# Batch 3's token sums by full-precision products, and batches 2 and 3 finished inside the first pair

## The chip, the cores and the metric

The kernel runs on one core of one Trainium2 chip. The metric is the device time of one execution in microseconds, median over runs. A core has five engines with a queue each: TensorE (PE in the rows, its weight loads PEld), VectorE (DVE), ScalarE (ACT), GpSimd (POOL), and SyncE (SP), which here issues the transfers. Each engine runs its own instructions strictly in program order and waits on semaphores.

## What is computed

An attention-like stage made of two int8-style quantised products adds to the residual `x`; then comes a mixture of experts in which the whole launch picks two of eight experts:

```python
x = x + xattn(layernorm(x), fside, ctx)      # x: 4 batches x 512 tokens x 512
n = layernorm(x).reshape(-1, 512)            # 2048 tokens
router_logits = n @ gate_w.T                 # 8 experts
_, sel = top_k(router_logits.sum(axis=0), 2) # ONE choice for all tokens
rw = softmax(router_logits[:, sel], axis=1)
h = gelu(einsum('nd,kdf->knf', n, w1[sel]) + b1[sel])
y = einsum('knf,kfd->knd', h, w2[sel]) + b2[sel]
x = x + einsum('nk,knd->nd', rw, y)
```

The choice needs the sum of all 2048 normalised tokens, and no expert weight can be fetched before it.

## The kernel before

Everything is written out by hand: for each engine a list of calls in the order in which its queue holds them. There is no scheduler.

**First stage** (to about 130 us): the quantised products of the four batches, b = 0 to 3. Then, per batch, second-layernorm moments (`moments(b, 2)`), the inverse root and minus mean times root on GpSimd (`inv_std`, L337), and four normalised tiles of 128 tokens: batch 2's by GpSimd (`normalise(2)`, L393), of batch 3 two by ScalarE and two by VectorE (`normalise_last`). TensorE transposes them (`normed2(b, h)`, 8 transposes of 128x128 each, L656) into PSUM slots `y.b.h`. Draining a slot also yields that batch's token sums, by an accumulating copy on ScalarE (`keep_full`) or by a reduction on VectorE (`token_sums`, L1334). `keep_hi` and `keep_lo` (L973, L1291) split the transposed batch into two rounded parts, whose sum is exact enough for three-product matmuls.

**Choice**: `token_total` (L1342) adds the sums of all batches; `expert_sums` (L677, 4 full-precision products with a right side of 8 columns) and `choose_experts` (L1346 to L1349) give `top_i`. SyncE reads it and issues the load of the first weights (L285, L289). ScalarE and VectorE split them (`first_weights`: a_hi L985, a_lo L1381), `pick_experts` and `pick_bias` (L1353 to L1375) select bias columns. `router(b)` (L667, 8 products of 512 columns) gives batch b's logits.

**Pairs**: an expert's hidden layer is cut into 8 parts; 16 pairs (expert, part) follow. Each handles the tokens in two halves, tp = 0 (batches 0, 1) and tp = 1 (batches 2, 3). In the first pair each half has four tiles `plain(tp, n)` (12 products each, L850), gelu on ScalarE, its low part on GpSimd (L476), and four `down` groups (12 products each, L805), drained by VectorE with the routing weights `rw` (L1541). In half 0 the logits of all batches are turned (`logit_columns`, L685) between tile 1 and tile 2; from them VectorE and GpSimd make `rw` (`pick_logits`, the power at L523, `token_weights`). Later pairs use a seven-product scheme (L792); they are not touched.

PSUM slots are handed on by a written table, `SLOT_USES`: a use may be filled when the use before it in its row is drained.

Of the kernel before, what the change touches and what calls it, by code (L numbers as in the profile page):

```python
# [14 lines left out]
P = 128  # L15
# [8 lines left out]
def xattn_ffn(  # L24
# [37 lines left out]
    with ExitStack() as ctx:  # L62
# [6 lines left out]
        def each(name):  # L69
# [43 lines left out]
        tok_sum = sb("tok_sum", [P, KD, B])  # L113
# [114 lines left out]
        part_ready, tok_ready, t4_sum = each("part_ready"), sem("tok_ready"), sem("t4_sum")  # L228
# [89 lines left out]
        def _(pool):  # L318
# [24 lines left out]

            def emptied(use):
                i, n = place(use)
                pool.wait_ge(drained[i], n + 1)
# [46 lines left out]
            def normalise(b):  # L393
                pool.wait_ge(nmr_ready[b], 2)
                for j in range(TT):
# [73 lines left out]
            normalise(2)  # L469
            inv_std(3, 2)  # L470
# [70 lines left out]
        def _(pe):  # L541
# [105 lines left out]
            def normed2(b, h):  # L647
                ps, full = fill(f"y.{b}.{h}")
                for j in range(TT):
                    if b == B - 1 and j >= H:  # L650
                        pe.wait_ge(xn_last, j - H + 1)
                    else:
                        pe.wait_ge(xn2_ready[b], j + 1)
# [18 lines left out]

            def expert_sums():
                pe.wait_ge(tok_ready, 1)
# [100 lines left out]
            normed2(3, 0)  # L775
            normed2(3, 1)
            router(1)
            expert_sums()
            router(0)
            router(2)  # L780
            router(3)
# [73 lines left out]
            def first_pair():  # L855
                for tp in range(2):
# [3 lines left out]
                    plain(tp, 0)  # L860
                    plain(tp, 1)
                    if tp == 0:
                        pe.wait_ge(drained[1], ALL_DRAINED[1])
                        for b in range(B):
                            logit_columns(b)
                    plain(tp, 2)
# [22 lines left out]
        def _(act):  # L889
            s = nc.scalar  # L890

            def normalise(b, c):
                act.wait_ge(nmr_ready[b], c)
                for j in range(H if c == 2 and b == B - 1 else TT):
                    s.activation(xv[b][:, j, :], res[:, b * TT + j, :], ACT.Identity, bias=nmr[c - 1][b][:, j:j + 1],
                                 scale=rstd[c - 1][b][:, j:j + 1]).then_inc(xn_ready[b] if c == 1 else xn2_ready[b], 1)

# [67 lines left out]
            def keep_summed(b, h):  # L965
                ps, empty = drain(f"y.{b}.{h}")
                act.wait_ge(part_ready[b], 1)
# [110 lines left out]
            keep_full(1, 1)  # L1078
            keep_hi(1, 0)
            keep_hi(1, 1)  # L1080
            keep_hi(0, 0)
            keep_hi(0, 1)
            normalise(3, 2)
            keep_full(2, 0)
            keep_full(3, 0)
            keep_summed(2, 1)
            keep_hi(2, 0)
            keep_hi(2, 1)
            keep_summed(3, 1)
            keep_hi(3, 0)  # L1090
            keep_hi(3, 1)
# [5 lines left out]
            keep_logits(2)  # L1097
            keep_logits(3)
# [527 lines left out]
```

## Time and profile before

| | us |
|---|---|
| median of 3 runs | 820.6 (820.12, 820.6, 821.82) |
| span of the profiled execution | 818.7 |
| TensorE busy in it | 771.5 (94%) |
| VectorE, GpSimd, ScalarE busy | 477.7, 449.7, 354.6 |
| mean granted TensorE clock | 0.979 |

The profiled execution's own device time is not listed apart from the three runs; its span, from first to last instruction, is 1.9 us under their median. Busy shares are means over stages with different limits: TensorE is 94% busy over the whole, but in the last 10 us before the choice of experts it is not. The change touches only the stretch from about 128 to 177 us.

### The profile page before, as it was taken

The page shows a single profiled execution, that of the slowest core. Times are in us where ns is not written, and L with a number is a line of the kernel's source. Part 1 is how long each engine was busy: PE and PEld are TensorE (multiplying, and loading weights), DVE is VectorE, ACT ScalarE, POOL GpSimd, SP SyncE. Part 2 cuts the span into 40 slices and gives each one's busy share as a digit, 9 for nine tenths or more (in the row PEclk, how much of TensorE's full clock was granted, in tenths as well). Part 3 has the DMA queues.
Part 4 walks back from the last instruction along what each step waited for, and adds up shares of the span by engine and source line. Part 5 has one row for each costly group of instructions (what it writes and reads, how often), then busy time and mean ns, then how long its engine had stood idle before and what let it go on. Part 6 is the DMA issues. An engine that isn't in the chain of part 4 may idle for free.

```text
span 818.7 us, 11342 instructions
## 1 busy us (share of the span) xinstructions
PE 771.5 (94%) x3570; PEld 624.1 (76%) x3577; DVE 477.7 (58%) x669; ACT 354.6 (43%) x660; POOL 449.7 (55%) x497
## 2 busy tenths in 40 slices
PE   5688666999999999999999999999999999999998
PEld 4666455688788888888888888888888888888886
DVE  5999759797754545454545454545454545454545
ACT  3967588743442434343424343434343434242422
POOL 1789997157564646464646464646464646464622
PEclk9899968999999999999999999999999999999999
DMA  9400000301010101010101010101010101010022
GB/s 344 173 2 1 1 0 2 129 1 51 1 52 1 51 0 49 3 50 2 48 4 51 1 45 6 42 9 44 7 41 11 36 15 36 15 32 19 0 103 104
DMA packets 19077, 32.34 MB, mean 39 GB/s; under 512 B 872, under 2 KB 11240, under 8 KB 18160
## 3 DMA queue, kind: packets, MB, share of 16 engines
q1 hardware_dynamic: 18896, 31.98, 11.1%
q8 instruction: 12, 0.20, 0.1%
q10 hardware_dynamic: 160, 0.08, 0.0%
q14 instruction: 9, 0.07, 0.0%
HBM read 27.87 MB, written 4.19 MB: 39 GB/s over the span
## 4 chain that ended last, share of the span: by engine, by line
PE 83%; POOL 8%; DVE 3%; issue 2%; ACT 2%; DMA 1%; ACTq 0%; POOLq 0%; DVEq 0%
PE slot L805 42%; PE slot L792 34%; PE slot L850 3%; POOL wv L366 2%; POOL xf L383 1%; PE slot L667 1%; POOL wv L372 1%; POOL cv L366 1%; PE slot L585 1%; DVE rmax L1226 1%; DMA b_rows<-in_L_ffn_b 1%; POOL rstd L340 1%; POOL h_lo L476 1%; DVE stats L1217 1%; DVE peak_x L1226 1%
## 5 line engine op out<-in xcount | busy, mean ns | idle before, releaser
L792 PE MATMUL slot<-xo,a_hi 128*128 128x512 f32 x840 | 259.1, 390 | 0.0
L1541 DVE SCALAR_TENSOR_TENSOR res<-slot,rw,res 128x512 f32<-128x512 f32 x256 | 178.5, 750 | 130.3 <-PE slot L805 130.2
L1570 DVE TENSOR_TENSOR e<-slot,e 128x512 f32<-128x512 f32 x150 | 103.8, 692 | 173.4 <-PE slot L792 173.3
L805 PE MATMUL slot<-w_hi,h_hi 128*128 128x512 f32 x512 | 201.3, 393 | 0.4 <-POOL h_lo L476 0.4
L805 PE MATMUL slot<-w_lo,h_hi 128*128 128x512 f32 x512 | 199.6, 390 | 0.0
L805 PE MATMUL slot<-w_hi,h_lo 128*128 128x512 f32 x512 | 199.4, 390 | 0.0
L792 PEld LDWEIGHTS slot<-xo,a_hi 128*128 128x128 f32 x840 | 157.4, 188 | 33.3 <-DVE e L1570 0.2
L476 POOL TENSOR_TENSOR h_lo<-e,h_hi 128x512 fp32r<-128x512 f32 x96 | 138.1, 1451 | 55.0 <-ACT e L1104 54.0
L792 PE MATMUL slot<-xo,a_lo 128*128 128x512 f32 x420 | 163.7, 390 | 0.0
L805 PEld LDWEIGHTS slot<-w_hi,h_hi 128*128 128x128 f32 x512 | 96.1, 188 | 25.1 <-POOL h_lo L476 5.6
L476 POOL TENSOR_TENSOR h_lo<-hid,h_hi 128x512 fp32r<-128x512 f32 x32 | 44.1, 1378 | 124.7 <-ACT hid L1104 124.7
L805 PEld LDWEIGHTS slot<-w_hi,h_lo 128*128 128x128 f32 x512 | 96.2, 188 | 20.1
L805 PEld LDWEIGHTS slot<-w_lo,h_hi 128*128 128x128 f32 x512 | 96.2, 188 | 19.3
L792 PEld LDWEIGHTS slot<-xo,a_lo 128*128 128x128 f32 x420 | 78.9, 188 | 16.5
L1103 ACT ACTIVATE h_hi<-e,b_now 128x512 fp32r<-128x512 f32 x90 | 64.9, 721 | 58.0 <-DVE e L1570 57.6
L1142 ACT COPY e<-slot 128x512 f32<-128x512 f32 x30 | 17.6, 587 | 164.5 <-PE slot L792 164.5
L490 POOL TENSOR_TENSOR a_lo<-raw,a_hi 128x256 fp32r<-128x256 f32 x45 | 34.3, 761 | 95.9 <-ACT a_hi L988 95.9
L991 ACT CAST w_hi<-raw 128x512 fp32r<-128x512 f32 x32 | 19.8, 622 | 109.8 <-PE slot L805 109.8
L495 POOL TENSOR_TENSOR w_lo<-raw,w_hi 128x512 fp32r<-128x512 f32 x30 | 38.7, 1289 | 50.4 <-ACT w_hi L991 50.4
L1104 ACT ACTIVATE e<-e,b_now 128x512 f32<-128x512 f32 x90 | 63.8, 709 | 0.0
L1103 ACT ACTIVATE h_hi<-slot,b_now 128x512 fp32r<-128x512 f32 x38 | 26.2, 689 | 66.5 <-PE slot L792 56.6
L490 POOL TENSOR_TENSOR a_lo<-ssum,a_hi 128x256 fp32r<-128x256 f32 x60 | 43.7, 739 | 0.0
(145 smaller groups left out, 814.5 us busy)
## 6 DMA issues: line engine op xcount, KB each, us to landing
raw<-in_L_ffn_w SPq DMA_DIRECT2D x32, 512.0 KB, 3.4
res<-in_x SPq DMA_DIRECT2D x4, 1024.0 KB, 11.9
wv<-in_fside_BxS2xS SPq DMA_DIRECT2D x4, 1024.0 KB, 12.8
out_x<-res SPq DMA_DIRECT2D x3, 1024.0 KB, 3.9
cv<-in_ctx SPq DMA_DIRECT2D x4, 512.0 KB, 13.1
out_x<-res SPq DMA_DIRECT2D x4, 256.0 KB, 2.7
b_row<-in_L_ffn_b SPq DMA_DIRECT2D x2, 256.0 KB, 4.6
b_rows<-in_L_ffn_b ACTq DMA_DIRECT2D x1, 64.0 KB, 6.0
```

What stands on the lines that cost most here:

```text
L366: g.tensor_tensor(w[:, j, :], w[:, j, :], rows[b][:, 0:n], ALU.mult).then_inc(wmul_ready[b], 1)
L476: g.tensor_tensor(h_lo[:, i, :], hid[i][:, :], h_hi[:, i, :].bitcast(F32), ALU.subtract).then_inc(h_ready, 1)
L490: g.tensor_tensor(a_lo[:, i, :, :], A_OF[i], a_hi[:, i, :, :].bitcast(F32), ALU.subtract).then_inc(a_ops_ready, 1)
L495: g.tensor_tensor(w2_lo[:, f, :], raw2[:, f, :], w2_hi[:, f, :].bitcast(F32), ALU.subtract).then_inc(w2_ready, 1)
L792: last = t.matmul(dst, a[:, i, k, :], xo[tp][:, v, k, :], start=(start and n == 0), stop=(n == 3 * H - 1), skip_group_check=True)
L805: last = t.matmul(y_bank[j][:, :], a[:, i, j * P:(j + 1) * P], v[:, f, :], start=(start and n == 0), stop=(not start and n == 2), skip_gro ...
L850: last = t.matmul(TILE_BANK[n], a[:, 2 * f + h, k, :], xo[q][:, v, k, :], start=(m == 0), stop=(m == 3 * KD - 1))
L991: s.copy(w2_hi[:, f, :], raw2[:, f, :]).then_inc(w2_hi_ready, 1)
L1103: s.activation(h_hi[:, i, :], src, ACT.Gelu_apprx_tanh, bias=bias).then_inc(hid_ready, 1)
L1104: s.activation(hid[i][:, :], src, ACT.Gelu_apprx_tanh, bias=bias).then_inc(hid_ready, 1)
L1541: v.scalar_tensor_tensor(out=r, in0=y_bank[j][:, :], scalar=rw[:, ds(p, 1), n:n + 1].rearrange("p a b -> p (a b)"), in1=r, op0=ALU.mult, o ...
L1570: v.tensor_tensor(dst[:, :], src, other[:, :], ALU.add).then_inc(comb_ready, 1)
```

## The change

1. Batch 3's token sums no longer wait for its transposes. The sum over tokens of (residual x root − mean x root) is formed by `last_sums`: for each of 4 token tiles and 4 feature blocks one full-precision product with the residual block as the stationary side and the column of roots as the moving side (16 products of 1 column, L697 in the new file), and one product of ones with the shifts (L694).
2. Batch 3's moments and roots come in two halves (`moments_last`, `inv_std_last`). Of batch 2's normalised tiles GpSimd makes two, ScalarE the other two (`normalise_half`).
3. `normed2(3, *)`, `router(2)` and `router(3)` move from before the choice into half 0 of the first pair; `logit_columns` moves behind `router(3)`, one tile later. The drains, splits and copies that belong to them move too on ScalarE and VectorE.
4. VectorE picks experts and bias, and normalises its two tiles of batch 3, before the first weights' low parts instead of after them.

```diff
- "a.2 s2.0 p2.0.1 y.3.1 r.3 "),
+ "a.2 s2.0 p2.0.1 t e r.1 "),
...
+def inv_std_last(h):
+    b, at = B - 1, slice(H * h, H * h + H)
+    pool.wait_ge(var_ready[b], 2 + h)
+    g.tensor_tensor(rstd[1][b][:, at], var_e[1][b][:, at], neg_half[:, at], ALU.pow).then_inc(rstd_last, 1)
+    pool.wait_ge(rstd_last, h + 1)
+    g.tensor_tensor(nmr[1][b][:, at], nmean[1][b][:, at], rstd[1][b][:, at], ALU.mult
+                    ).then_inc(nmr_ready[b], 1)
...
-def normalise(b):
+def normalise(b, h):
     pool.wait_ge(nmr_ready[b], 2)
-    for j in range(TT):
+    for j in range(H * h, H * h + H):
...
 inv_std(2, 2)
-normalise(2)
-inv_std(3, 2)
+normalise(2, 0)
+inv_std_last(0)
+inv_std_last(1)
...
+        elif b == B - 2 and j >= H:
+            pe.wait_ge(xn_acts, j - H + 1)
...
+def last_sums(h):
+    b = B - 1
+    ps, full = fill("t") if h == 0 else (slot[place("t")[0]], filled[place("t")[0]])
+    pe.wait_ge(rstd_last, h + 1)
+    for j in range(H * h, H * h + H):
+        if h == 1 and j == TT - 1:
+            pe.wait_ge(nmr_ready[b], 3)
+            t.matmul(ps[:, 0, KD:2 * KD], ones[:, :], nmr[1][b][:, :], start=True, stop=True,
+                     skip_group_check=True)
+        for k in range(KD):
+            last = t.matmul(ps[:, 0, k:k + 1], res[:, b * TT + j, k * P:(k + 1) * P],
+                            rstd[1][b][:, j:j + 1], start=(j == 0), stop=(j == TT - 1),
+                            skip_group_check=True)
+    if h == 1:
+        last.then_inc(full, 1)
 def expert_sums():
-    pe.wait_ge(tok_ready, 1)
     ps, full = fill("e")
     for k in range(KD):
...
-normed2(3, 0)
-normed2(3, 1)
-router(1)
+last_sums(0)
+last_sums(1)
 expert_sums()
 router(0)
-router(2)
-router(3)
+router(1)
...
         plain(tp, 0)
+        if tp == 0:
+            normed2(3, 0)
+            normed2(3, 1)
         plain(tp, 1)
         if tp == 0:
             pe.wait_ge(drained[1], ALL_DRAINED[1])
+            router(2)
+        plain(tp, 2)
+        if tp == 0:
+            router(3)
             for b in range(B):
                 logit_columns(b)
-        plain(tp, 2)
         pe.wait_ge(hid_ready, 8 + 8 * tp + 2)
         plain(tp, 3)
...
+def normalise_half(b):
+    act.wait_ge(nmr_ready[b], 2)
+    for j in range(H, TT):
+        s.activation(xv[b][:, j, :], res[:, b * TT + j, :], ACT.Identity, bias=nmr[1][b][:, j:j + 1],
+                     scale=rstd[1][b][:, j:j + 1]).then_inc(xn_acts, 1)
...
-    act.wait_ge(part_ready[b], 1)
+    if b == 2:
+        act.wait_ge(part_ready, 1)
...
+keep_hi(0, 0)
+normalise_half(2)
+keep_hi(0, 1)
+keep_full(2, 0)
 keep_hi(1, 0)
 keep_hi(1, 1)
-keep_hi(0, 0)
-keep_hi(0, 1)
 normalise(3, 2)
-keep_full(2, 0)
-keep_full(3, 0)
 keep_summed(2, 1)
-keep_hi(2, 0)
-keep_hi(2, 1)
-keep_summed(3, 1)
-keep_hi(3, 0)
-keep_hi(3, 1)
 keep_logits(0)
 keep_logits(1)
 first_weights(0, 2)
 first_weights(2, 4)
 s.activation(gelu_warm[:, :], half[:, 0:1], ACT.Gelu_apprx_tanh)
-keep_logits(2)
-keep_logits(3)
-first_down_weights()
+keep_hi(2, 0)
+keep_hi(2, 1)
...
             gelu(0, n, TILES[n][0], TILE_BANK[n])
+            if tp == 0 and n == 0:
+                keep_summed(3, 0)
+                keep_summed(3, 1)
+            if tp == 0 and n == 1:
+                keep_hi(3, 0)
+                keep_hi(3, 1)
+                first_down_weights()
+                keep_logits(2)
+            if tp == 0 and n == 2:
+                keep_logits(3)
...
+def moments_last(h):
+    b, at = B - 1, slice(H * h, H * h + H)
+    for j in range(H * h, H * h + H):
+        if h == 0:
+            dve.wait_ge(res_added[b], j + 1)
+        else:
+            dve.wait_ge(res_last, j - H + 1)
+        ins = v.bn_stats(stats[b][:, j, :], res[:, b * TT + j, :])
+    link(ins)
+    for j in range(H * h, H * h + H):
+        ins = v.bn_aggr(mv[b][:, j, :], stats[b][:, j, :])
+    link(ins)
+    v.tensor_scalar(nmean[1][b][:, at], mv[b][:, at, 0], -1.0, None, ALU.mult)
+    v.tensor_scalar(var_e[1][b][:, at], mv[b][:, at, 1], LN_EPS, None, ALU.add).then_inc(var_ready[b], 1)
...
+def early_total():
+    for b in range(B - 1):
         emptied(f"y.{b}.0")
     for b in range(2):
         emptied(f"y.{b}.1")
-        dve.wait_ge(part_ready[2 + b], 1)
-    v.tensor_reduce(tok_total[:, :], tok_sum[:, :, :], AX.X, ALU.add).then_inc(tok_ready, 1)
+    dve.wait_ge(part_ready, 1)
+    link(v.tensor_reduce(tok_early[:, :], tok_sum[:, :, :], AX.X, ALU.add))
+def token_total():
+    ps, empty = drain("t")
+    link(v.tensor_reduce(tok_shift[:, :], ps[:, 0, KD:2 * KD], AX.X, ALU.add))
+    v.scalar_tensor_tensor(out=tok_total[:, :], in0=ps[:, 0, 0:KD], scalar=tok_shift[:, 0:1],
+                           in1=tok_early[:, :], op0=ALU.add, op1=ALU.add).then_inc(empty, 1)
...
 moments(2, 2)
+moments_last(0)
 add_last_residual()
-moments(3, 2)
+moments_last(1)
+token_sums(2)
+early_total()
 keep_lo(0, 0)
-keep_lo(1, 0)
-normalise_last()
-token_sums(2)
-keep_lo(1, 1)
-token_sums(3)
 token_total()
 keep_lo(0, 1)
 choose_experts()
+normalise_last()
+keep_lo(1, 0)
+keep_lo(1, 1)
+pick_experts()
+pick_bias()
+first_weights(0, 2)
+first_weights(2, 4)
 keep_lo(2, 0)
 keep_lo(2, 1)
-keep_lo(3, 0)
-keep_lo(3, 1)
-first_weights(0, 2)
-first_weights(2, 4)
-pick_experts()
-pick_bias()
-first_down_weights()
-pick_logits()
...
     last_operands(0)
+    keep_lo(3, 0)
+    keep_lo(3, 1)
+    first_down_weights()
     fourth_operand(0)
+    pick_logits()
     token_weights()
```

Three places of the written order follow. First TensorE, from the end of batch 2's transposes to the choice: before, in this piece, batch 3's last transposes (slot1), `router(1)` and the expert product.

```order
L656 MATMUL slot1<-ident,xf1 128x128 [waits xn_last]
L656 MATMUL slot1<-ident,xf1 128x128
L667 MATMUL slot2<-xo0,gwt 16x512 [waits lo_ready1,drained2]
L667 MATMUL slot2<-xo0,gwt 8x512
...
L677 MATMUL slot3<-gwt_full,tok_total 128x8 [waits drained3,tok_ready]
L677 MATMUL slot3<-gwt_full,tok_total 128x8 x3
```

And now, at the same place (L697 and L694 are `last_sums`, L706 the expert product, L681 `router(0)`):

```order
L697 MATMUL slot1<-rstd2_3,res 128x1 [waits rstd_last,drained1]
L697 MATMUL slot1<-rstd2_3,res 128x1 x7
L697 MATMUL slot1<-rstd2_3,res 128x1 [waits rstd_last]
L697 MATMUL slot1<-rstd2_3,res 128x1 x3
L694 MATMUL slot1<-nmr2_3,ones 128x4 [waits nmr_ready3]
L697 MATMUL slot1<-rstd2_3,res 128x1 x4
L706 MATMUL slot1<-gwt_full,tok_total 128x8 [waits drained1]
L706 MATMUL slot1<-gwt_full,tok_total 128x8 x3
L681 MATMUL slot0<-xo0,gwt 16x512 [waits lo_ready0,drained0]
```

The transposes of batch 3 and one router are gone from ahead of the expert product, and 17 products stand there.

Second, VectorE between the choice (MAX_INDEX writes `top_i`) and the first weights' low parts (`a_lo`), before:

```order
L1349 MAX_INDEX top_i<-top_v,sum_row 128x8 [waits dve_link]
L1291 TENSOR_TENSOR xo1<-xf1,xo1 128x1024 [waits hi_ready2] x2
L1291 TENSOR_TENSOR xo1<-xf1,xo1 128x1024 [waits hi_ready3] x2
L1381 TENSOR_TENSOR a_lo<-raw1,a_hi 128x256 [waits a_hi_ready] x4
L1353 CAST top_f<-top_i 128x8 [waits top_ready]
```

and now:

```order
L1414 MAX_INDEX top_i<-top_v,sum_row 128x8 [waits dve_link]
L1382 TENSOR_SCALAR xf1<-res,rstd2_3,nmr2_3 128x512 [waits nmr_ready3]
L1382 TENSOR_SCALAR xf1<-res,rstd2_3,nmr2_3 128x512
L1350 TENSOR_TENSOR xo0<-xf0,xo0 128x1024 [waits hi_ready1] x2
L1418 CAST top_f<-top_i 128x8 [waits top_ready]
L1420 TENSOR_SCALAR onehot<-iota,top_f 128x16 [waits dve_link] x2
L1438 TENSOR_TENSOR picked<-b1_all,onehot 128x16x8 [waits dve_link]
L1440 TENSOR_REDUCE b1_col<-picked 128x16 [waits dve_link]
L1438 TENSOR_TENSOR picked<-b1_all,onehot 128x16x8 [waits dve_link]
L1440 TENSOR_REDUCE b1_col<-picked 128x16 [waits dve_link]
L1446 TENSOR_TENSOR a_lo<-raw1,a_hi 128x256 [waits dve_link,a_hi_ready]
```

Four splits stood there; now two normalised tiles, two splits (`keep_lo(1, *)`, which `router(1)` needs) and seven small instructions stand there.

Third, TensorE in half 0 of the first pair, behind its first tile (L877 is `plain`, L670 `normed2(3, *)`, L681 `router(2)`, L714 `logit_columns`), now:

```order
L877 MATMUL slot0<-xo0,a_lo 128x512
L670 MATMUL slot2<-ident,xf1 128x128 [waits xn2_ready3,drained2]
...
L877 MATMUL slot0<-xo0,a_hi 128x512 [waits lo_ready0,a_ops_ready]
...
L681 MATMUL slot2<-xo1,gwt 16x512 [waits lo_ready2,drained2,drained1]
...
L877 MATMUL slot1<-xo0,a_hi 128x512 [waits lo_ready1,a_ops_ready]
...
L681 MATMUL slot3<-xo1,gwt 16x512 [waits lo_ready3,drained3]
...
L714 MATMUL slot1<-ident,logits 128x16 [waits drained3]
```

Before, only the logit columns stood between the tiles of this half.

## Rows read from the trace of the kernel before

**Rows 1.** The page: shares of the chain that ended last, by engine.

```profile
PE 83%; POOL 8%; DVE 3%; issue 2%; ACT 2%; DMA 1%; ACTq 0%; POOLq 0%; DVEq 0%
```

**Rows 2.** Chain of waits, 136 to 177 us: start us, us, what.

```profile
136.63 1.94 POOL rstd L340
...
139.89 3.87 PE slot L656 x16
143.75 2.79 PE slot L667 x8
...
147.34 1.87 PE slot L667 x8
...
149.29 2.14 PE slot L667 x8
...
153.71 5.47 PE slot L850 x24
...
160.28 5.69 PE slot L850 x24
165.97 10.88 PE slot L805 x48
```

**Rows 3.** Windows, TensorE alone: stretch, length, busy, granted clock.

```profile
132.00:135.40 3.40, 0.66 (x4) 1.00 0.00 0
135.40:138.80 3.40, 3.00 (x14) 0.51 0.00 0
138.80:142.20 3.40, 2.59 (x12) 0.50 0.01 2
142.20:145.60 3.40, 3.40 (x13) 0.50 0.00 0
```

**Rows 4.** The same view of an earlier stretch.

```profile
16.00:19.40 3.40, 3.31 (x16) 0.50 0.99 387
```

**Rows 5.** Timeline of TensorE: start us, us, engine line op out<-in xcount.

```profile
123.27 1.09 PE L656 MATMUL slot<-ident,xf 128*128 128x128 f32 x8
...
135.90 3.18 PE L656 MATMUL slot<-ident,xf 128*128 128x128 f32 x12 [0.30 <-POOL xf L396]
...
139.89 3.87 PE L656 MATMUL slot<-ident,xf 128*128 128x128 f32 x16 [0.81 <-ACT xf L895]
...
146.38 0.95 PE L677 MATMUL slot<-gwt_full,tok_total 128*128 128x8 f32 x8
```

**Rows 6.** Timeline of VectorE, 138 to 157 us.

```profile
138.93 1.00 DVE L1323 TENSOR_SCALAR xf<-res,rstd,nmr 128x512 f32<-128x512 f32 x2
...
145.24 1.22 DVE L1291 TENSOR_TENSOR xo<-xf,xo 128x1024 fp32r<-128x1024 f32 x1
...
147.86 0.16 DVE L1349 FIND_INDEX8 top_i<-top_v,sum_row 128x8 uint32<-128x8 f32 x1
...
152.60 1.43 DVE L1381 TENSOR_TENSOR a_lo<-raw,a_hi 128x256 fp32r<-128x256 f32 x4
153.95 0.17 DVE L1353 CAST top_f<-top_i 128x8 f32<-128x8 uint32 x1
...
155.84 0.29 DVE L1375 TENSOR_REDUCE b_col<-picked 128x16 f32<-128x128 f32 x1
```

**Rows 7.** Timeline of ScalarE, 133 to 155 us.

```profile
133.00 3.89 ACT L973 CAST xo<-xf 128x1024 fp32r<-128x1024 f32 x4
138.93 1.52 ACT L895 ACTIVATE xf<-res,nmr,rstd 128x512 f32<-128x512 f32 x2 [2.04 <-POOL nmr L341]
...
149.24 1.05 ACT L982 COPY logits<-slot 16x512 f32<-16x512 f32 x2 [0.30 <-PE slot L667]
152.16 1.33 ACT L985 CAST a_hi<-raw 128x256 fp32r<-128x256 f32 x4 [1.87 <-DMA raw<-in_L_ffn_w]
```

**Rows 8.** Timeline of GpSimd: the power for the routing weights.

```profile
162.69 2.90 POOL L523 TENSOR_TENSOR lpow<-euler,lsub 128x16 f32<-128x16 f32 x1 [0.84 <-DVE lsub L1366]
```

**Rows 9.** Timeline of VectorE: the first outputs with routing weights.

```profile
170.07 2.73 DVE L1541 SCALAR_TENSOR_TENSOR res<-slot,rw,res 128x512 f32<-128x512 f32 x4
```

More of the change, by code:

```diff
@@ L112, in xattn_ffn @@
         logits = sb("logits", [2 * E, B, T])
-        tok_sum = sb("tok_sum", [P, KD, B])
+        tok_sum = sb("tok_sum", [P, KD, B - 1])
+        tok_early = sb("tok_early", [P, KD])
+        tok_shift = sb("tok_shift", [P, 1])
         tok_total = sb("tok_total", [P, KD])
@@ L227, in xattn_ffn @@
         res_last, xn_last = sem("res_last"), sem("xn_last")
-        part_ready, tok_ready, t4_sum = each("part_ready"), sem("tok_ready"), sem("t4_sum")
+        part_ready, t4_sum = sem("part_ready"), sem("t4_sum")
+        rstd_last, xn_acts = sem("rstd_last"), sem("xn_acts")
         tsum_ready = [sem(f"tsum_ready{tp}") for tp in range(2)]
@@ L1320, in normalise_last @@
                 b = B - 1
-                dve.wait_ge(nmr_ready[b], 2)
+                dve.wait_ge(nmr_ready[b], 3)
                 for j in range(H, TT):
@@ L1333, in token_sums @@
                 ps, _ = drain(f"y.{b}.1")
-                v.tensor_reduce(tok_sum[:, H:2 * H, b], ps[:, :, :], AX.X, ALU.add).then_inc(part_ready[b], 1)
-            def token_total():
-                for b in range(B):
+                v.tensor_reduce(tok_sum[:, H:2 * H, b], ps[:, :, :], AX.X, ALU.add).then_inc(part_ready, 1)
+            def early_total():
+                for b in range(B - 1):
                     emptied(f"y.{b}.0")
```

6 rows, old and new, of the table SLOT_USES are left out of this document.

## The prediction, on record before the result

> **What bounds the kernel now.** I read the page first: the chain that ended last lies on TensorE for 83% of the span [rows 1]. So work on TensorE counts wherever it does not fall into a gap. The chain in order of time comes next [rows 2]. The reader is to see three pieces. Until 139.89 us the chain is on GpSimd: batch 3's inverse root, 136.63 to 138.57, and then the normalised tiles that wait for it. From 139.89 to 153.71 it is all TensorE: 16 transposes of batch 3, router(1), the expert product, the other three routers. From 153.71 to 176.85 it is TensorE again: the four tiles of the first pair's half 0 and its four down groups. In this last piece nothing else shows, so what is moved into it lengthens it by its full duration.
>
> Third, the clock [rows 3]. TensorE was granted its full 2.4 GHz until 135.4, fell to 1.2 GHz after a stretch in which it worked 0.66 of 3.40 us, and stayed there to 145.6, although it was busy for 3.00, 2.59 and 3.40 us of the three stretches that follow. Batch 3's transposes therefore cost 3.87/16 = 0.242 us each [rows 5], against 1.09/8 = 0.136 at full clock.
>
> Fourth, how the first weights arrive. The choice is known at 147.86 + 0.16 = 148.02 [rows 6], the weights are there and ScalarE starts on them at 152.16 [rows 7], 4.14 us later, and the low parts start at 152.60. A first tile could start at about 153.3; router(3) ends at 153.71. So weights and TensorE are late together, by 0.4 us, and to gain anything both must come earlier.
>
> **The change, step by step.** I follow the path to the first tile (call its start W), then what is put behind it.
>
> *Batch 2's transposes.* Now GpSimd makes four tiles and the last transposes run to 135.90 + 3.18 = 139.08 [rows 5]. ScalarE takes two of them behind one split of 3.89/4 = 0.97 us from 133.00, at 1.52/2 = 0.76 each: ready at 135.5 instead of 136.6 [rows 7]. Twelve transposes at 0.242 from about 135.4 end at 138.3. Gain 0.8 us.
>
> *Batch 3's roots.* VectorE makes the second half's moments about 1 us later than now, GpSimd has two tiles fewer ahead; the power took 1.94 us for four columns [rows 2] and cannot take longer for two, so the roots are there by 138.9. TensorE is in the first half of the sums until later than that. No wait.
>
> *The token sums.* 16 + 1 full-precision products. The expert product shows the kind: 4 products are 8 records and 0.95 us, 0.119 us a pass at full clock [rows 5]; at half clock I take the 0.242 of a transpose, which also loads 128 columns. 34 passes are 4.0 us at full clock and 8.2 at half. This is the disputed price. At full clock from the start the sums end at 142.4, at half to the end at 146.5. Which clock? The rows speak both ways: in an earlier stretch TensorE did nothing but transposes for 3.3 of 3.4 us at half clock [rows 4] and was at full clock right after it; from 135.4 to 143.7 it did transposes nearly without a pause and was not [rows 3]. No row shows a stream of 1-column products. I take the middle, a clock that comes back halfway: 6.1 us, end at 144.4.
>
> The Trainium skill (TensorE: Matmul & The Clock Gate, Why this matters for your kernels) says that keeping TensorE continuously busy is what brings the full clock. By that rule the sums, which are dense, run at full clock nearly from their start, the first of the rivals below; rows 4 agree with it, the stretch 138.8 to 143.7 in rows 3 does so poorly. The same page (LDWEIGHTS) lets a weight load cost its columns, whatever the product behind it is: 128 columns give 107 ns, so that 34 loads would be an estimated 3.6 us for products of a single column. The 0.119 us a pass beside an 8-column product agrees. It speaks against this form of the sum: with the residual as the stationary side the cost is all loading.
>
> *From the sums to the choice.* Two small VectorE instructions with their gaps, 0.45: 144.9. Expert product 0.95: 145.8. From there to the index the row of before needs 148.02 − 147.33 = 0.7 [rows 5, 6]: 146.5. Against 148.02 that is 1.5 us earlier. The weights land 4.14 later, at 150.7.
>
> *From the choice to the first tile.* The weights are not what comes last now. VectorE's queue holds ahead of the first low part: batch 3's two tiles 1.00, two splits of 1.22, and the picks, 153.95 to 156.13 or 2.2 us [rows 6]; together 5.6 us, to 152.1. Behind them two low parts at 1.43/4 = 0.36, and a semaphore: W = 153.0. On ScalarE the high parts wait behind the logits of router(1), whose operands VectorE has ready at 150.0; router 2.14 us at most [rows 2], copy 0.5, high part 0.33 [rows 7]: also 152 to 153. So W comes 0.7 us earlier than 153.71, and 5.6 us of VectorE's list eat the earlier choice.
>
> *What is moved behind W.* 16 transposes at 0.136: 2.2 us, if the clock is full there. Two routers at 2.14 [rows 2]: 4.3 us. Logit columns wait for the copy of the last logits, 1.05/2 = 0.52 [rows 7] and two hand-overs, while before they had been drained: 0.6. Sum 7.1 us. Cover: none, the chain there is TensorE without a break.
> The batch 3 drains, splits and copies now in ScalarE's and VectorE's lists run beside tiles 1 and 2 and the routers (2 x 2.14 + 2 x 2.73 us); their sum on ScalarE is about 6 us with a gelu of 1.3 between. Cost nothing, 0.5 at most if router(3) waits for its low part. GpSimd's low parts of the hidden tiles stand ahead of later down groups and have time.
>
> *Routing weights.* Logit columns stand one tile later. From the end of the columns at 160.28 to the first output at 170.07 it took 9.8 us [rows 2, 9], of which the power is 2.90 [rows 8]. TensorE needs the first drained bank after a tile and two down groups, 5.69/2 + 10.88/2 = 8.3 us, less now than before (11.1). VectorE has no operand sums left between pick and weights, which cost over 3 us there; I take 7.9 to 9.4 and a stall of 0.2 (0 to 1.1).
>
> **Sum.** Start of down: 153.0 + (165.97 − 153.71 = 12.26) + 7.1 = 172.4, against 165.97: +6.4. With the stall +6.6. SyncE's queue has the same entries. Nothing later is touched: the chain goes on with 10.88 us of down groups and follows TensorE. Span 818.7 + 6.6 = 825.3; the median stands 1.9 above the span, so 820.6 + 6.6 = 827.2; I say 827.0.
>
> **Rivals.**
> *R1, full clock through the sums.* They end at 142.5 to 142.8, W at 151.3, the rest as above: +4.7, 825.3. For it: rows 4, and less waiting ahead of batch 2's last transposes. Against it: three stretches of rows 3.
> *R2, half clock until the routers.* Sums 8.2 us, expert product 1.9: the choice at 149.6, later than before, so the change doesn't do what it says; W = 156.1, and the first tile may still run slowly. +9.7, 830.3. For it: in rows 3 the clock came back only once routers had run for over 2 us (from 143.7), and now nothing wide runs between 138.3 and the choice. Against it: rows 4.
> *R3, not slower.* Mechanism: the early choice pays in full. Choice at 142.1 with the clock never lost, the landing 4.14 later rather than VectorE's list setting W, and low parts at once: W = 147.0, +0.4 net of the 7.1: 821.0 or, with no wait for logits, 820.4. It decides from W below 153.71 − 7.1 = 146.6. VectorE's 5.6 us of list speak against it, and they are in the written order.
> *R4, another wait,* such as router(3) behind its split or the third down group behind the weights by more than 1 us: +1 to +2 on any of these.
>
> **How the numbers follow.** About 0.2% (1.6 us) is what a measurement here tells from no change. Forecast (clock back within the sums) 0.42; R1 0.22; R2 0.26; R3 0.08, half of it below −1.6 us or so through something not seen; R4 alone 0.02. The forecast's own range is 825.3 to 829. The whole range must take in R1 and most of R2: 823.5 to 831. Slower 0.92, same 0.04, faster 0.04.
>
> **What would show it.** The granted clock from 138 to 146, and the length of the block of 1-column products: 4.0, 6.1 or 8.2 us. The index at 146.5, the first a_lo at about 152.2 with its wait on VectorE's own queue and not on the transfer. W near 153. Then in half 0 transposes of 2.2 us and two routers of 2.1 us on the chain, between the tiles, and the down groups from 172.4. Wrong would be: a chain that leaves TensorE in half 0, sums under 4 us, or W below 150.

## The result, and the profile after

| | before | after |
|---|---|---|
| median of 4 runs each, us | 821.21 (820.12 to 821.84) | 827.39 (826.95 to 829.17) |
| span of the profiled execution, us | 818.7 | 825.4 |
| TensorE busy in it, us | 771.5 | 776.5 |
| mean granted TensorE clock | 0.979 | 0.977 |

The change is slower: ratio 1.0089, 95% interval [1.0076, 1.0103]. The medians stand 6.2 us apart, which alone would be 1.0075, at the lower end of the interval; the spans of the two profiled executions stand 6.7 apart. In a second set of runs the ratio was 1.0105 [1.0083, 1.0126].

The shares of the chain are nearly those of [rows 1]; VectorE has gained a point, and we will see where:

```profile
PE 82%; POOL 8%; DVE 4%; issue 3%; ACT 2%; DMA 1%; ACTq 0%; POOLq 0%; DVEq 0%
```

The chain of waits of the changed kernel over the stretch of [rows 2] (start us, us, what):

```profile
135.98 3.16 PE slot L670 x14
139.14 2.82 PE slot L697 x24
...
143.59 1.88 PE slot L706 x8
145.47 5.75 PE slot L681 x16
...
152.87 2.99 PE slot L877 x12
155.86 1.75 PE slot L670 x16
...
160.35 1.85 PE slot L681 x8
...
164.94 1.85 PE slot L681 x8
166.78 1.11 PE slot L714 x16
...
170.36 2.91 POOL lpow L535
...
176.86 0.76 DVE res L1603
177.76 5.70 PE slot L832 x24
```

Read it against [rows 2] at two places. The first tile of the pair starts at 152.87 instead of 153.71: that is the whole yield of the early choice, 0.84 us. Its half 0 now holds 1.75 us of transposes and 1.85 + 1.85 us of routers. The down groups start at 170.7 instead of 165.97. And the chain leaves TensorE behind the logit columns (L714): it reaches the third down group over GpSimd's power and VectorE's small steps to `res`. Before, it did not.

Windows of TensorE in the changed kernel (stretch, length, busy and count, granted clock), to stand beside [rows 3]:

```profile
135.40:138.80 3.40, 2.82 (x14) 0.61 0.03 5
138.80:142.20 3.40, 3.40 (x30) 0.89 0.01 2
142.20:145.60 3.40, 2.89 (x17) 0.61 0.00 0
145.60:149.00 3.40, 3.40 (x9) 0.50 0.23 60
```

The full clock came back at about 139.5, early in the block of sums, and was lost again at about 142.9, although TensorE had been busy for all of 138.8 to 142.2. So the 8 records of the expert product took 1.88 us instead of the 0.95 of [rows 5], and `router(0)` began at 1.2 GHz.

Timeline of TensorE after, the wait at the third down group (in brackets the idle time ahead and what ended it):

```profile
177.76 0.47 PE L832 MATMUL slot<-w_hi,h_hi 128*128 128x512 f32 x1 [1.45 <-DVE res L1603]
```

TensorE waits here for a bank that VectorE drains with the routing weights. The row shows 1.45 us of idle time. But the end of a product's record overlaps with the start of the next. Two down groups take 5.44 us, half of the 10.88 in [rows 2], so the third was due at 170.70 + 5.44 = 176.14 and started 1.62 us late; 1.62 is the figure used below. Timeline of VectorE after, to stand beside [rows 6, 9]:

```profile
145.99 0.16 DVE L1414 FIND_INDEX8 top_i<-top_v,sum_row 128x8 uint32<-128x8 f32 x1
...
152.16 1.43 DVE L1446 TENSOR_TENSOR a_lo<-raw,a_hi 128x256 fp32r<-128x256 f32 x4 [0.76 <-ACT a_hi L1025]
...
173.36 1.27 DVE L1581 TENSOR_TENSOR lexp<-lpow,is_top 128x16 f32<-128x16 f32 x2 [2.91 <-POOL lpow L535]
174.55 1.26 DVE L1582 TENSOR_SCALAR lden<-lpow 128x16 f32<-128x16 f32 x1
```

And of GpSimd:

```profile
173.22 2.56 POOL L488 TENSOR_TENSOR h_lo<-e,h_hi 128x512 fp32r<-128x512 f32 x2
```

`lexp` (two instructions) and `lden` work on 128x16 values. The first `lexp` took 0.16 us, the second 1.18 and `lden` 1.26. They lie exactly beside two low parts (`h_lo`) on GpSimd, subtractions with two inputs, 1.28 us each.

This hold-up is not new. The kernel before has it too, though TensorE did not wait there (timelines of VectorE and of GpSimd before; L1295 and L1310 are operand sums):

```profile
162.82 2.49 DVE L1295 TENSOR_TENSOR xf<-xf 128x1024 f32<-128x1024 f32 x2
165.34 1.23 DVE L1310 TENSOR_TENSOR xf<-xf 128x1024 f32<-128x1024 f32 x1
166.60 1.24 DVE L1519 TENSOR_TENSOR lexp<-lpow,is_top 128x16 f32<-128x16 f32 x2
167.76 1.26 DVE L1520 TENSOR_SCALAR lden<-lpow 128x16 f32<-128x16 f32 x1
```

```profile
165.56 3.43 POOL L476 TENSOR_TENSOR h_lo<-e,h_hi 128x512 fp32r<-128x512 f32 x2
```

### The profile page after: what moved, and what is told of

It reads as the page before. It is cut to its first block, busy times and chain, and to the rows that moved or that the text cites. A ratio compares the mean times of both kernels' runs of the same rounds, so it can differ in the third digit from the quotient of the medians.

```text
span 825.4 us, 11412 instructions
## 1 busy us (share of the span) xinstructions
PE 776.5 (94%) x3604; PEld 629.5 (76%) x3611; DVE 477.9 (58%) x672; ACT 355.5 (43%) x659; POOL 448.6 (54%) x497
## 4 chain that ended last, share of the span: by engine, by line
PE 82%; POOL 8%; DVE 4%; issue 3%; ACT 2%; DMA 1%; ACTq 0%; POOLq 0%; DVEq 0%
PE slot L832 41%; PE slot L819 33%; PE slot L877 2%; POOL wv L377 2%; PE slot L681 1%; POOL xf L394 1%; POOL wv L383 1%; POOL cv L377 1%; DVE rmax L1285 1%; PE slot L597 1%; DMA b_rows<-in_L_ffn_b 1%; POOL h_lo L488 1%; PE slot L670 1%; DVE stats L1261 1%; DVE peak_x L1285 1%
```

## The experiments

After the prediction's result three things were open: whether the wait for the routing weights is what the rows suggest; what decides TensorE's clock around the sums; and which part of the change costs the 6 us. Every ratio below is against the kernel before, run on the same chip in the same set. That kernel's median was 821.21, 819.47, 820.01 and 819.87 us in the four sets, so times of different sets are compared by their ratios.

### Low part ahead of the power

In `first_pair` on GpSimd:

```diff
                 hid_lo(0, 0, 1)
+                hid_lo(0, 0, 2)
                 pool.wait_ge(lsub_ready, 1)
                 g.tensor_tensor(lpow[:, :], euler[:, :], lsub[:, :], ALU.pow).then_inc(lexp_ready, 1)
-                hid_lo(0, 0, 2)
+                pool.wait_ge(y_free, TT + 1)
                 hid_lo(0, 0, 3)
```

> The changed kernel with one edit on GpSimd: the third hidden tile's low part goes ahead of the power for the routing weights, the fourth waits until the first output of the pair is drained, so that nothing of GpSimd's runs beside VectorE's small instructions that make the weights. Theory (the wait of the third down group is made by GpSimd's two subtracts running beside lexp and lden, 1.27 and 1.26 us instead of about 0.3 each): the weights are ready 1.8 us earlier, TensorE's gap before the third down group (176.1 to 177.8) closes, and the kernel gains 1.6 us: 825.8. Rival (those two instructions are slow of themselves, or the power alone is late): the gap stays, 827.4, or 1 us worse since the fourth low part now comes late.

Measured: 825.76 us, ratio 1.0073 [1.0056, 1.009], against 1.0089 and 1.0105 of the changed kernel. VectorE's timeline:

```profile
174.90 0.26 DVE L1582 TENSOR_TENSOR lexp<-lpow,is_top 128x16 f32<-128x16 f32 x2 [2.91 <-POOL lpow L536]
175.07 0.17 DVE L1583 TENSOR_SCALAR lden<-lpow 128x16 f32<-128x16 f32 x1
```

With nothing beside it on GpSimd, `lden` takes 0.17 us, not 1.26, and TensorE waits nowhere between 165 and 190. The intervals of the ratios overlap, so the times alone would not prove the gain; that the wait is gone, and why, the trace shows.

### The block of sums twice

```diff
             last_sums(0)
+            last_sums(1, False)
+            last_sums(0)
             last_sums(1)
```

The 17 added products compute the same sums once more.

> The changed kernel with batch 3's sums formed twice in a row on TensorE (17 full-precision products more, the same result). It prices the block and shows its clock. Theory A (weight loads beside 1-column products do not keep the full clock, it was lost at 142.8 after 3.4 us of them): the first block runs as before, the second wholly at half clock, 34 passes x 0.24 = 8 us, and the time rises by about 8 us, 835.5. Theory B (a busy TensorE keeps its clock): 34 x 0.12 = 4 us, 831.4, granted clock 1.0 from 139.4 on.

Measured: 835.99 us, ratio 1.0199 [1.018, 1.0218]; the span is 7.7 us longer than the changed kernel's (833.1 against 825.4), as theory A had it. Timeline and windows of TensorE:

```profile
139.47 2.98 PE L697 MATMUL slot<-rstd,res 128*128 128x1 f32 x24
142.53 6.20 PE L697 MATMUL slot<-rstd,res 128*128 128x1 f32 x32
...
149.03 1.84 PE L697 MATMUL slot<-rstd,res 128*128 128x1 f32 x8
```

```profile
142.20:145.60 3.40, 3.40 (x23) 0.67 0.00 0
145.60:149.00 3.40, 3.40 (x17) 0.50 0.00 0
149.00:152.40 3.40, 2.89 (x14) 0.50 0.00 0
```

The first 24 records cost 0.124 us each, the last 8 cost 0.230: 1.2 GHz. The clock came back at about 140.0, within the first block, and was lost at about 143.4, just before the second block began (about 143.6). TensorE was busy without a break on both sides of that moment, so a pause there is not what takes the clock away. The second block, with the expert product behind it, did not win it back: all stretches from 145.6 to 155.8 show 0.50.

### Two wide products between the sums

```diff
             last_sums(0)
+            for _ in range(2):
+                t.matmul(slot[0][0:16, 0, :], ident[:, 0:16], res[:, 0, :], start=True, stop=True)
             last_sums(1)
```

The added products fill a free bank; nothing reads them.

> The changed kernel with two full-precision products of 512 columns put between the two halves of batch 3's sums (their result is overwritten). They cost about 0.85 us each by themselves. Theory A (only wide products keep the clock): the clock stays at 1.0 through the expert product and router(0), which then take 0.95 and 1.9 us instead of 1.88 and 3.4, so the 1.7 us spent come back and the time is within 0.7 us of the changed kernel's 827.4. Rival (the loss at 142.8 has another reason): the clock falls all the same and the time is 1.7 us more, 829.

Measured: 828.11 us, ratio 1.011 [1.009, 1.013]. Windows of TensorE:

```profile
142.20:145.60 3.40, 2.92 (x20) 1.00 0.00 0
145.60:149.00 3.40, 3.37 (x14) 0.62 0.00 0
```

The two products cost 1.89 us and the first tile starts 0.7 us later in the trace (153.59 instead of 152.87): some of the price came back as clock (the expert product took 1.21 us, not 1.88). By the ratios the kernel can't be told from the changed one. The clock fell all the same, at about 146.4 instead of 142.9, in the expert product that follows the rest of the sums. So the wide products put the loss off; they did not prevent it.

One trace of each kernel would be thin evidence for this. But the stretch from 142.2 to 145.6 shows 0.59 to 0.73 in all six traces in which the clock came back during the sums and nothing wide stands between them (both executions of the changed kernel, the first two experiments, the sums alone, the mended orders), and 1.00 in the two with wide products between.

### The sums alone

Part 1 of the change as it is, and batch 3's transposes and all routers ahead of the pair, as before; the pair itself is the old one. On TensorE:

```diff
             expert_sums()
-            router(0)
+            normed2(3, 0)
+            normed2(3, 1)
+            router(0)
             router(1)
+            router(2)
+            router(3)
```

> Part 1 of the change alone: batch 3's sums by products and the early choice stay, but transposes of batch 3 and all four routers stand ahead of the first pair again, behind the expert product, with their drains and splits; the pair is as in the kernel before. Theory (5.5 us of moved work has no cover in the pair, and the later logit columns make the 1.6 us wait): TensorE works through from the choice to about 156.8 and starts the tiles there, the down groups start at 169.1, no wait behind them: +3.1 on the kernel before, 824.3, so 3.2 us faster than the changed kernel. Rival (the place of that work does not matter, the sums are what costs): about 827.4 as well. Rival 2 (the move was worth it): above 828.

Measured: 824.36 us, ratio 1.0058 [1.0042, 1.0075]. Chain of waits:

```profile
139.62 2.80 PE slot L697 x24
...
145.94 3.51 PE slot L670 x16
149.44 7.79 PE slot L681 x32
157.23 5.45 PE slot L881 x24
...
169.45 10.88 PE slot L836 x48
```

By the ratios as they stand (1.0058 against 1.0089 and 1.0105) more than half of the loss stays. The sums and the expert product now stand ahead of the same transposes and routers as before, and the transposes still run at half clock (3.51 us for 16). All of it is TensorE's own work, one piece behind the other, so no earlier choice can shorten it: the first tile starts at 157.23 instead of 153.71. VectorE's `lexp` and `lden` are held up here too (1.24 and 1.26 us), yet TensorE waits nowhere between 157 and 190: the logit columns stand one tile earlier again.

### A router between the halves of the sums

The kernel above, with `router(0)` between `last_sums(0)` and `last_sums(1)`, and VectorE's splits for it ahead of batch 2's token sums.

```diff
             last_sums(0)
+            router(0)
             last_sums(1)
             expert_sums()
...
-            router(0)
```

> The kernel with the sums alone (824.4) with useful wide work between the two halves of the sums: router(0), 8 products of 512 columns, whose low parts VectorE makes before it needs to reduce batch 2. Theory A (1-column products lose the full clock, wide ones hold it): the clock stays at 1.0 from where it comes back, the expert product takes 0.95 instead of 1.88, batch 3's transposes 2.0 instead of 3.5, and the tiles start 2.8 us earlier: 821.6. Rival (the clock falls by something else): the order alone saves nothing, 824.4, or the choice 1 to 2 us later makes the weights late, 825 to 826.

Measured: 823.07 us over 12 runs, ratio 1.0043 [1.0026, 1.0059]; this overlaps with the interval of the sums alone. The tiles start at 155.84 instead of 157.23. Windows:

```profile
142.20:145.60 3.40, 3.05 (x23) 1.00 0.00 0
145.60:149.00 3.40, 3.24 (x19) 0.67 0.00 0
```

It repeats the picture of the two wide products, now with useful ones: full clock while they run, the expert product 1.06 us instead of 1.88, then half clock again for batch 3's transposes (3.46 us for 16 in the chain of waits, 3.51 with the sums alone).

### The changed kernel again, and high parts ahead of the logits

The changed kernel unaltered, as a measure of how it repeats:

> The changed kernel itself once more, as the anchor for the others of this set: 827.4 by its first runs, and the same lengths in the trace: sums 4.0 us, clock lost some 3.5 us after it came back.

Measured: 828.72 us, ratio 1.0105 [1.0083, 1.0126], with the same wait of 1.6 us at the third down group. And with one line of ScalarE's list moved:

```diff
-            keep_logits(1)
             first_weights(0, 2)
             first_weights(2, 4)
+            keep_logits(1)
```

> The changed kernel with the first weights' high parts (a_hi, ScalarE) ahead of the copy of router(1)'s logits. Theory (the low parts waited 0.76 us for a_hi, which stood behind that copy; the transfer had landed at about 150.3): the first tile starts 0.7 us earlier and so does all behind it, 826.7. Rival (the transfer or VectorE's own list set the start): no change, 827.4.

Measured: 828.27 us, ratio 1.0104 [1.0077, 1.0131]; no gain is shown. Its profiled execution shows something else, in TensorE's windows:

```profile
135.40:138.80 3.40, 3.40 (x18) 0.50 0.01 2
138.80:142.20 3.40, 3.40 (x17) 0.50 0.00 0
142.20:145.60 3.40, 3.20 (x15) 0.50 0.00 0
```

Up to the sums this kernel is the changed kernel, instruction by instruction, yet here the clock did not come back before the routers: 4.91 us for the first 24 records instead of 2.82 (chain of waits), index at 148.30, first tile at 154.56. With the index that late VectorE's own list sets the first tile, so this trace can't show what the moved line is worth. It is the course of rival R2, met in one execution, at 829.0 us. So the clock in this stretch is not fixed by the program alone, and runs of the changed kernel spread from 827.0 to 829.7.

### Three written orders mended

The changed kernel with the low part ahead of the power (as in the first experiment), the high parts ahead of the logits, and VectorE's `first_weights` ahead of the picks:

```diff
-            pick_experts()
-            pick_bias()
             first_weights(0, 2)
             first_weights(2, 4)
+            pick_experts()
+            pick_bias()
```

> The changed kernel with three orders changed together: GpSimd's low parts around the power as in the first experiment, ScalarE's a_hi ahead of router(1)'s logits, and VectorE's first low parts ahead of the picks of experts and bias. Theory (VectorE's list and the copy of the logits, not the transfer, set the first tile; GpSimd's subtracts make the wait for the routing weights): 1.3 us at the first tile and 1.6 behind it, 2.9 us less than the changed kernel, ratio to before about 1.006. Rival (the arrival of the weights sets the first tile): the 1.6 us alone, ratio 1.0075.

Measured: 824.96 us, ratio 1.0067 [1.005, 1.0084]. Chain of waits:

```profile
147.26 3.44 DMA raw<-in_L_ffn_w
...
151.85 3.01 PE slot L878 x12
```

Now the transfer sets the first tile: 151.85, 1.0 us earlier than in the changed kernel, and the wait for the routing weights (1.6 us) is gone too. By the two traces the written orders cost the change some 2.6 us. What is left, 1.0067, can't be told from the 1.0058 of the sums alone: with its orders mended, finishing batches 2 and 3 inside the pair shows neither a loss nor a gain against doing it ahead of the pair.

### The kernel before, with the clock held

Four products that nothing reads, in TensorE's empty stretch behind `normed2(1, 1)`:

```diff
             normed2(1, 1)
+            emptied("p2.0.1")
+            for _ in range(4):
+                t.matmul(slot[1][0:16, 0, :], ident[:, 0:16], res[:, 0, :], start=True, stop=True)
             normed2(2, 0)
```

> The kernel before with four full-precision products of 512 columns (3.6 us, result unused) in TensorE's empty stretch of 3.4 us ahead of batch 2's transposes. Theory A (the half clock of 135.4 to 145.7 comes from that empty stretch and costs the transposes of batch 3 1.8 us and router(1) 0.9 us on the path): the clock stays at 1.0, the tiles start 2.5 us earlier, the time is 2.4 us less than the kernel before, ratio 0.997. Rival (the path there is set by GpSimd's root and the arrival of weights, not TensorE's clock): no change, or 0.3 us more.

Measured: 819.28 us over 12 runs, ratio 0.999 [0.9974, 1.0005]: no gain is shown. The clock stayed at 1.00 to 142.2, but TensorE then waited for GpSimd:

```profile
133.97 4.09 POOL L396 TENSOR_SCALAR xf<-res,rstd,nmr 128x512 f32<-128x512 f32 x4
```

The four tiles took 3.05 us in the kernel before. Here three took 0.77 each and the last one 1.84, beside a split on VectorE with two inputs. So batch 3's transposes started at 141.26 instead of 139.89 and ended at 144.05 instead of 143.75, though at full clock 14 of them took 2.18 us where 16 had taken 3.87: GpSimd's lateness took what the clock gave back. The profiled execution (821.5 us) is one of the three longest of the twelve; the other nine lie between 818.1 and 819.7, and no trace shows what they gained. That GpSimd's tiles and the root behind them set the path is what the next experiment tries.

### The kernel before, with half of batch 2's tiles on ScalarE

The piece of the change that takes two tiles off GpSimd, alone:

```diff
-                for j in range(TT):
+                for j in range(H):
...
             keep_full(1, 1)
+            keep_hi(0, 0)
+            normalise_half(2)
             keep_hi(1, 0)
             keep_hi(1, 1)
-            keep_hi(0, 0)
             keep_hi(0, 1)
```

> The kernel before with one piece of the change: of batch 2's four normalised tiles ScalarE makes two, so that GpSimd comes to batch 3's root sooner. Nothing else is changed. Theory (ahead of the choice the path before runs over GpSimd: four tiles of 3.05 us, then the root, 1.94 us beside VectorE's splits): the root is ready about 1 us earlier, batch 3's transposes start at 138.8 instead of 139.9, and the kernel is 1.0 to 1.2 us faster than before, ratio 0.9987. Rival (TensorE at half clock is the bound from 136 on, since batch 2's transposes end only at 138.3): 0.5 us or nothing.

Measured: 817.55 us (817.28 to 820.45, 11 runs) against 819.87 (23 runs), ratio 0.9979 [0.9967, 0.9992]. This beats both kernels, by a little. Chain of waits:

```profile
135.60 1.91 POOL rstd L341
...
137.87 1.53 ACT xf L898 x2
...
139.44 1.75 PE slot L659 x14
141.19 1.85 PE slot L670 x8
...
162.72 10.88 PE slot L808 x48
```

Windows of TensorE:

```profile
135.40:138.80 3.40, 2.49 (x12) 0.66 0.00 0
138.80:142.20 3.40, 3.17 (x22) 1.00 0.01 2
```

Batch 3's root starts at 135.60 instead of 136.63 [rows 2]. In this execution the clock is back by 138.8, 14 of the transposes take 1.75 us where 16 took 3.87, and the down groups start at 162.72 instead of 165.97. Not all of these 3.2 us are the edit's: about half a microsecond stands ahead of it (batch 2's root starts at 131.33 instead of 131.80), and the medians are 2.3 us apart. That the earlier tiles are what brings the clock back is likely, not shown; there is one trace of each kernel. With the four unread products added, the clock is full from 132 to 152.4:

> The same with four full-precision products of 512 columns in TensorE's empty stretch, whose result is not used. Theory (with GpSimd out of the way the held clock pays: batch 3's transposes 2.1 instead of 3.9 us, router(1) 1.9 instead of 2.8): another 2 us, 3 us faster than before, ratio 0.9965. Rival (the full clock is lost again in the thin transposes behind, as in the version with the held clock alone, where it fell at 143): 1 to 1.5 us faster at most, ratio 0.9985.

Measured: 817.64 us over 12 runs, ratio 0.9978 [0.9967, 0.999]: nothing more. In both traces the clock was there for batch 3's transposes (1.75 us for 14).

## Why the prediction was right, point by point

- *What bounds.* Right for TensorE's own work: nearly all that was put into the pair lengthened the chain. But the prediction named as signs of being wrong "a chain that leaves TensorE in half 0, sums under 4 us, or W below 150". The chain did leave TensorE in half 0, and the sums took 3.96 us.
- *Batch 2's transposes* end at 139.1, not 138.3. The half that GpSimd still makes took it 2.46 us from 133.47: its second tile took 1.71 us instead of 0.76, beside VectorE's residual additions with two inputs (from 133.65, 1.72 us), which had stood earlier in the kernel before. So the tiles were all there only at 135.9; the prediction had timed ScalarE's half alone. The gain of 0.8 us fell away.
- *Roots in time:* right, the second half of the sums waited for nothing.
- *The sums:* 4.0 us (139.14 to 143.10), the lower bound, where 6.1 was taken from the middle. That was rival R1's price. But R1 needed the clock to stay, and the expert product, at half clock, gave 0.9 us of it back. The late transposes (0.8) and the slow expert product (0.9) nearly make up for the 2.1 us that the sums were cheaper: the index was there at 146.15, expected at 146.5. The execution with half clock throughout shows that such a course is real too, but cheaper than the upper bound: 7.1 us for the whole block (138.35 to 145.41), not 8.2, because a pass of such a load costs 0.21 us there and not the 0.242 of a transpose.
- *First tile:* 152.87, predicted 153.0, and not because of VectorE's list alone. The first `a_lo` waited 0.76 us for ScalarE's high part, which stood behind `router(1)`'s logits. Both lists were named as ending between 152 and 153. VectorE's list took 5.3 us from the index (146.15 to 151.41), predicted 5.6.
- *What is moved:* 1.75 + 1.85 + 1.85 = 5.45 us, predicted 7.1. The 2.14 us of a router in [rows 2] held a short wait for the splits, the 0.136 of a transpose was 0.109 here, and the 0.6 for the columns did not arise.
- *Routing weights:* the step that failed. The prediction took 7.9 to 9.4 us from the end of the columns to the first output, set 8.3 us of TensorE's work against it and got a stall of 0.2 (0 to 1.1). The stall was 1.62. The first output started 9.0 us behind the columns (167.87 to 176.86), inside the range, and TensorE needed 8.25. But TensorE waits for a drained bank and not for an output that has started: that output took 0.76 us and the hand-over to TensorE 0.14, and these 0.9 us stand in no term. The reason given, that "VectorE has no operand sums left between pick and weights, which cost over 3 us there", was wrong too. Those sums ran mostly beside the power, which ended at 165.59 in the kernel before; they ended at 166.57 and so cost 1.0 us on this path. The larger piece, `lexp` and `lden` held up beside GpSimd's low parts, is in both kernels, and no term names it; the first experiment takes that company away and the stall with it. It became a stall only now because the columns stand one tile later: with the sums alone, where they stand in the old place, the same hold-up makes no wait.
- *Rivals.* The stall is what R4 named ("the third down group behind the weights by more than 1 us: +1 to +2 on any of these"), with a chance of 0.02 alone. What was met is R1's price for the sums, without the clock that R1 kept behind them, and R4's wait. R3's choice at 142.1 does not follow from the prediction's own terms: transposes, sums, expert product and index at full clock from 135.4 end at about 143.2. The rival's total would be 1.1 us later, 822.1.
- *Sum:* −0.84 for the first tile, +5.45 moved, +1.62 stall are 6.2 of the 6.7 measured; of the rest about 0.4 lies in the tiles and down groups of half 0, which ends at 183.46 instead of 176.85. 6.6 was predicted. A moved piece too dear by 1.6 and a stall too cheap by 1.4 made one correct total. That the total fits this closely is luck; that the change is slower, and by several microseconds, is not: it follows from the 5.45 us of work without cover.

Why the change is slower in substance: batch 3's token sums had been a by-product of drains on ScalarE and VectorE, beside TensorE. Now TensorE makes them, 34 weight loads on the engine that sets the end. With the rest in its old order (the sums alone) that costs more than half of the loss. The rest comes with the placing in the pair: what VectorE and ScalarE had time for between routers now meets the weights' splits and the routing weights. Mending the written orders takes out about that much (1.0067). What the sums alone lose against the kernel before was not taken apart further between the loads themselves and the clock behind them.

## What to carry to other kernels

An early decision is worth only what the next engine in line can use: ask what TensorE still owes at that moment, for work that it owes anyway sets the end in any order. A reduction that rides on a drain cost TensorE nothing here; the same sum as products with a 128-column stationary side was 34 passes and 4.0 us. When you move a wait, compare the two moments that meet in it: the end of the drain and the moment at which TensorE needs the bank. And before such a rebuild, try taking tiles off the engine that feeds the gap: here two tiles gave 0.2%, and the rebuild cost 0.9 to 1.0%.

## What the runs showed of the hardware

- *A busy TensorE can lose its full clock.* In the changed kernel it worked without a break from 139.14 to 143.1, in weight loads of 128 columns and products of one, got the full clock at about 139.5 and was at 1.2 GHz again from 142.9. With the block doubled the second one ran at 1.2 GHz throughout. With products of 512 columns between, the full clock lasted to 146.4 and, with a router between, to 146.7. What exactly decides is open: in the kernel before with the clock held, two stretches of 3.40 us in which TensorE worked 1.56 and 1.36 us kept 1.00, and the next, with 3.40 us of transposes and router, showed 0.62. The Trainium skill (TensorE: Matmul & The Clock Gate, Why this matters for your kernels) says to keep TensorE continuously busy for the full clock; for such loads and products this case's traces do not agree.
- *What such a pass costs.* 0.12 us at full clock (2.98 us for 24 records), 0.21 to 0.23 at half clock (5.12 for 24, 1.84 for 8, each by the timeline). The Trainium skill (TensorE: Matmul & The Clock Gate, LDWEIGHTS) gives 107 ns for a load of 128 columns: near the figure at full clock, half of the one at half clock.
- *VectorE and GpSimd hold each other up.* An instruction on 128x16 values took VectorE 0.17 us alone and 1.18 or 1.26 beside subtractions on GpSimd of 1.28 each. In turn one of GpSimd's tiles took 1.71 us (changed kernel) and 1.84 (clock held) beside additions or splits with two inputs on VectorE, and 0.76 without. The Trainium skill (SBUF — State Buffer, SBUF: two separate sides) describes a port pair that the two engines share under a lock which is held for a whole instruction; the traces agree in that the small instruction waits about as long as a large one of the other engine takes. `lden` has only one input; no run shows under which condition of that lock it falls.
- *The clock's course differs between executions.* The same 24 records of the sums took 2.82 us in one and 4.91 in another (chain of waits). A single trace of such a stretch shows one of several courses.
